# Turning the gathered rows of the expert part: TensorE and a copy from PSUM, or a transfer from tile to tile

## The chip, the core and the metric

The kernel runs on one core of a Trainium2 chip. The core has a matrix engine (TensorE, PE in the rows), three elementwise engines (VectorE or DVE, ScalarE or ACT, GpSimd or POOL), SyncE (SP), which here only issues transfers, and 16 DMA engines that carry out the transfers of all queues. Each engine runs its own instruction list in order; they meet through semaphores only. The metric is the device time of one execution in microseconds; lower is better.

## What is computed

One layer on 8 x 512 rows of 256 values: a modulated layer norm, a causal linear attention over 16 heads, a gated residual, a second modulated norm, and a mixture of 8 experts of which each row takes two. Cut to the part that matters here:

```
probs = softmax(xf @ router_w.T);  topv, topi = top_k(probs, 2);  topv = topv / (topv.sum() + 1e-9)
h   = gelu(einsum('td,edh->teh', xf, w1))        # D = 256, H = 1024, E = 8
y   = einsum('teh,ehd->ted', h, w2)
out = einsum('te,ted->td', cw, y)                # cw: the two shares of each row
x   = x + gb * out
```

## The kernel before

The kernel has two parts, one after the other. The first part (attention, second norm, router) walks over 32 chunks of 128 rows; it also splits each expert weight into a high and a low half of 16 bits, which stay in SBUF. It writes each normalised row, with its gate beside it, to `ffn_rows` in DRAM. A short piece between the parts sorts the rows by expert into `MAXB` = 71 blocks of 128 rows, each block of one expert.

The second, the expert part, runs 71 steps, one block each. For block m:

- GpSimd gathers 128 rows of `ffn_rows` into the slot `xg[q]` (8 slots, named `xt` and `stage` in the rows), 5 blocks ahead (`AHEAD`), and the shares with a second small gather.
- ScalarE's `row_high(m)` rounds the row's 256 values to 16 bits into `xs[:, m.p, 0:D]` (the tile `kstT`), VectorE's `row_low(m)` puts the remainder into `xs[:, m.p, D:2D]`. `m.p` is the parity of m: `xs` holds two blocks.
- TensorE's `xT(m)` transposes the four 128x128 pieces of it (`transpose_parts`, line 1172) into the PSUM bank `bank[7 * m.p]`; VectorE copies the bank to `x16[:, m.p, :]` (the tile `qstT`, line 716), two blocks as well.
- First product, W1 from here on (lines 1334 and 1336): 16 pairs of matmuls of 256 and 128 columns into `hidden`. ScalarE and VectorE add the parts, apply gelu and split the result in `amhi` and `amlo`.
- Second product, W2 (lines 1350 and 1352): 8 pairs of 512 and 256 columns. ScalarE and VectorE then form the gated row block, and GpSimd adds it into `out_dram` by an indirect transfer (line 919), each such transfer after the one before it has landed.

The order is written out by hand in `step_c` of each engine. TensorE's list in step a is `xT(a+1)`, W1(a), W2(a-1). Before W1(a) it waits for `xTe`, which VectorE raises after the copy of block a. VectorE's list in step a is: sum of W2(a-2), index copies, gated block a-2 (line 709), the copy of block a+1 (line 716), `row_low(a+2)` (line 687), two sums of W1(a) (line 723), two low halves (line 729). ScalarE's list is: the low part of W2(a-2), `row_high(a+2)`, two copies of W1(a), four gelus. ScalarE's `row_high(m)` waits for `xT` of block m-2, since it writes over that block's half of `xs`; VectorE's copy waits for `hB` of block m-2, the end of W1(m-2), since it writes over that block's half of `x16`. SyncE issues its last transfer, the shares to DRAM (line 1459), before the expert part begins and nothing in it.

Of the kernel before, what the change touches and what calls it, by code (L numbers as in the profile page):

```python
# [29 lines left out]
F16 = mybir.dt.float16  # L30
# [4 lines left out]
P = 128  # L35
B, S, D = 8, 512, 256
# [12 lines left out]
MAXB = (2 * T + E * (P - 1)) // P  # L49
# [51 lines left out]
def wait(eng, sem, value, most=None):  # L101

    if isinstance(value, int):
        if most is not None:
            value = min(value, most)
        if value <= 0:
            return
    eng.wait_ge(sem, value)


def adaln_block(nc, x, w_qkv, w_out, router_w, w1, w2, c_in, wmod, rope_cos, rope_sin, out):
    ctx = ExitStack()
    with ctx:
# [3 lines left out]
        def sem(name):  # L117
            return ctx.enter_context(nc.semaphore(name))
# [176 lines left out]
        s_g = [sem(f"s_g{q}") for q in range(GB)]  # L295
        s_h = [sem(f"s_h{q}") for q in range(GB)]
        s_shares = sem("s_shares")
        s_sc = sem("s_sc")

        x_rows = x.rearrange("b s d -> (b s) d")  # L300
# [21 lines left out]
        def steps_a(eng, step, order, after={}):  # L322


            for c in range(2 * CPB):
                step(At(0, c, CPB))
                if c in after:
                    after[c]()
            with eng.Fori(2, B - 1) as b:
                for c in range(CPB):  # L330
                    step(At(b, c, CPB))
            for c in range(CPB + max(lag for _, lag in order)):
                step(At(B - 1, c, CPB))

        def steps_c(eng, step):

# [58 lines left out]
        def _(dve):  # L395
# [289 lines left out]
            def row_low(m):  # L685
                wait(dve, c_["xh"], m.n + 1)
                v.tensor_tensor(xs[:, m.p, D:2 * D], xg[m.c % GB][:, 0:D], xs[:, m.p, 0:D], ALU.subtract)\
                    .then_inc(c_["xl"], 1)

            row_low(At(0, 0, UC))  # L690
            row_low(At(0, 1, UC))
            dve.wait_ge(c_["xT"], 1)
            v.tensor_copy(x16[:, 0, :], bank[0][:, 0:D].bitcast(F16)).then_inc(c_["xTe"], 1)

            def step_c(a):
                m = a.back(2)
# [8 lines left out]
                if m.inside(MAXB):  # L705
# [3 lines left out]
                    v.scalar_tensor_tensor(out=yw[:, m.p, :], in0=y_sum, scalar=share[:, q:q + 1],  # L709
                                           in1=xg[q][:, D:2 * D], op0=ALU.mult, op1=ALU.mult)\  # L710
                        .then_inc(c_["yw"], 1)
                m = a.back(-1)
                if m.inside(MAXB):
                    wait(dve, c_["xT"], m.n + 1)
                    wait(dve, c_["hB"], m.n - 1)
                    v.tensor_copy(x16[:, m.p, :], bank[7 * m.p][:, 0:D].bitcast(F16)).then_inc(c_["xTe"], 1)
                if a.back(-2).inside(MAXB):
                    row_low(a.back(-2))
                if a.inside(MAXB):
# [208 lines left out]
        def _(act):  # L928
# [108 lines left out]
            def row_high(m):  # L1037
                q, used = m.slot(GB)
                wait(act, s_g[q], 16 * (used + 1))
                wait(act, c_["xT"], m.n - 1)  # L1040
                copy(xs[:, m.p, 0:D], xg[q][:, 0:D]).then_inc(c_["xh"], 1)

            row_high(At(0, 0, UC))
# [27 lines left out]
        def _(pe):  # L1071
# [222 lines left out]
            last.then_inc(s_pe, 1)  # L1294


            def xT(m):
                wait(pe, c_["xl"], m.n + 1)
                wait(pe, c_["xTe"], m.n - 1)
                transpose_parts(bank[7 * m.p], xs[:, m.p, :]).then_inc(c_["xT"], 1)  # L1300

            pe.wait_ge(a_["whi"], NC)
            pe.wait_ge(a_["wlo"], NC)
            xT(At(0, 0, UC))
            pe.wait_ge(s_dve, marks["block_e"])

            expert, digits = {}, {}
# [6 lines left out]
            def step_c(a):  # L1314
# [3 lines left out]
                ahead = a.n + UC // 2  # L1318
                if ahead % UC == 0 and ahead < MAXB:
                    load_digits(ahead // UC)  # L1320
                if a.back(-1).inside(MAXB):
                    xT(a.back(-1))
                if a.inside(MAXB):
                    e = expert[a.n]
                    wait(pe, c_["xTe"], a.n + 1)
                    for mt in range(MT):
                        g, q = mt // 4, mt % 4
                        if q == 0:
# [32 lines left out]
        def _(sp):  # L1361
# [96 lines left out]
            sp.wait_ge(s_pool, marks["shares"])  # L1458
            sp.dma_start(share_d.rearrange("(p i) e -> p (i e)", i=NC), shares).then_inc(s_shares, 16)


# [1 line left out]
_INS = ["L0_attn_x", "L0_attn_w_qkv", "L0_attn_w_out", "L0_ffn_router_w", "L0_ffn_w1", "L0_ffn_w2",  # L1463
# [28 lines left out]
```

## Time and profile before

| | |
|---|---|
| median of 3 runs | 825.89 us (824.83 to 827.75) |
| the profiled execution | 825.53 us |
| its span in the trace | 823.2 us |
| TensorE busy | 737.3 us, 90% |
| VectorE, ScalarE, GpSimd busy | 81%, 71%, 62% |
| mean granted TensorE clock | 0.958 |

The span runs from the first to the last instruction of the trace; some 2.3 us of the execution lie outside it. The profile gives busy time by engine, and the same in 40 slices of the span, so that the two parts can be told apart: slices 1 to 18 are the first part, 19 and 20 the sorting, and 21 to 40 the expert part, from about 413 us on. A matmul is shown with the time from its start to its modelled end; several are under way at once, so that the distance between two starts, and not the duration, tells what one costs TensorE.

### The profile page before, as it was taken

The numbers are of one execution on the slowest core, as the hardware profiler recorded it, in microseconds if no ns is written. First come the engines' busy times: TensorE is split into PE (matmuls) and PEld (weight loads), VectorE is DVE, ScalarE is ACT, GpSimd is POOL, SyncE is SP. The second block draws the span as 40 slices with busy tenths as digits, with TensorE's granted clock in tenths as the row PEclk, the third lists the DMA queues.
The fourth block names the chain that finished last, engine by engine and source line by source line (L and its number), as shares of the span: only waits on it lengthen the run. The fifth ranks groups of instructions, "written<-read, shape, count | busy, mean of one in ns | idle before, by whom it ended". The sixth has DMA issues, their size and how long they took to land.

```text
span 823.2 us, 26404 instructions
## 1 busy us (share of the span) xinstructions
PE 737.3 (90%) x7949; PEld 540.3 (66%) x7949; DVE 663.8 (81%) x1488; ACT 580.3 (71%) x1103; POOL 514.3 (62%) x504
## 2 busy tenths in 40 slices
PE   6599999999999999973489999999999999999994
PEld 3366666666666666652367777777777777777772
DVE  2789999999999999965857777778777877777773
ACT  1478888888888888862057777777677767677762
POOL 3547576766666575744746666666676667667653
PEclk9799999999999999995589999999999999999998
DMA  6214333333333333310023333343334334343320
GB/s 207 86 41 126 107 115 111 107 108 105 111 113 114 109 116 115 112 53 32 21 79 75 73 71 69 68 78 70 73 73 76 66 69 78 66 76 70 74 31 0
DMA packets 52814, 68.78 MB, mean 84 GB/s; under 512 B 8864, under 2 KB 44080, under 8 KB 52736
## 3 DMA queue, kind: packets, MB, share of 16 engines
q0 software_dynamic: 18176, 27.06, 17.5%
q1 hardware_dynamic: 34560, 40.61, 16.0%
q8 instruction: 58, 0.95, 0.5%
q14 instruction: 20, 0.16, 0.1%
HBM read 46.50 MB, written 22.05 MB: 83 GB/s over the span
## 4 chain that ended last, share of the span: by engine, by line
PE 59%; DVE 16%; issue 10%; ACT 8%; POOL 3%; DMA 1%; DVEq 1%; another core or an unknown queue 0%; ACTq 0%; SPq 0%; POOLq 0%
PE hidden L1334 15%; PE bank L1350 15%; PE hidden L1336 8%; PE bank L1352 7%; PE bank L1189 5%; PE hidden L1172 3%; DVE amlo L511 2%; DVE nb L452 2%; PE bank L1172 2%; ACT feat L969 2%; ACT rb L968 2%; DVE rb L498 2%; DVE hT L475 2%; DVE st L432 2%; ACT qstT L932 1%
## 5 line engine op out<-in xcount | busy, mean ns | idle before, releaser
L1334 PE MATMUL hidden<-qstT,w1hi_k 128*128 128x256 f16 x1136 | 200.2, 274 | 1.1 <-DVE am L723 1.1
L1336 PE MATMUL hidden<-qstT,w1lo_k 128*128 128x128 f16 x1136 | 195.5, 220 | 0.0
L1350 PE MATMUL bank<-w,amhi 128*128 x568 | 188.6, 379 | 0.4
L1352 PE MATMUL bank<-w,amlo 128*128 x568 | 154.8, 273 | 0.0
L729 DVE TENSOR_TENSOR amlo<-am,amhi 128x512 f16<-128x512 f32 x142 | 98.4, 693 | 62.6 <-ACT am L1064 50.8
L919 POOL DMA_INDIRECT out_dram<-x,si x71 | 121.9, 1717 | 36.5 <-issue 27.4
L1334 PEld LDWEIGHTS hidden<-qstT,w1hi_k 128*128 x1136 | 111.7, 98 | 14.9 <-issue 1.3
L1336 PEld LDWEIGHTS hidden<-qstT,w1lo_k 128*128 x1136 | 111.7, 98 | 1.1
L1189 PE MATMUL bank<-wq,hT 128*128 128x256 f32 (+1 forms) x256 | 102.9, 528 | 9.2 <-DVE hT L475 9.1
L1063 ACT ACTIVATE amhi<-am 128x512 f16<-128x512 f32 x142 | 88.5, 623 | 12.6 <-DVE am L723 7.6
L1350 PEld LDWEIGHTS bank<-w,amhi 128*128 128x128 f16 x568 | 55.5, 98 | 62.3 <-issue 2.6
L1064 ACT ACTIVATE am<-am 128x512 f32<-128x512 f32 x142 | 87.5, 616 | 0.0
L900 POOL DMA_INDIRECT wq<-shares,gi x71 | 67.8, 955 | 22.1 <-issue 14.9
L511 DVE SCALAR_TENSOR_TENSOR amlo<-hidden,amhi 128x1024 f16<-128x1024 f32 x64 | 78.1, 1220 | 2.6 <-ACT amhi L994 2.3
L822 POOL CAST kst<-feat 128x512 f16<-128x512 f32 x32 | 19.5, 609 | 96.9 <-DVE feat L505 96.7
L932 ACT ACTIVATE feat<-hidden 128x512 f32<-128x512 f32 x71 | 42.4, 597 | 40.6 <-PE hidden L1336 36.3
L932 ACT ACTIVATE rb<-hidden 128x512 f32<-128x512 f32 x71 | 42.5, 598 | 38.8 <-PE hidden L1336 37.7
L1189 PEld LDWEIGHTS bank<-wq,hT 128*128 128x128 f32 x256 | 45.6, 198 | 36.3 <-issue 15.9
L994 ACT ACTIVATE amhi<-hidden 128x1024 f16<-128x1024 f32 x64 | 65.0, 1015 | 3.0 <-PE hidden L1135 1.5
L892 POOL DMA_INDIRECT xt<-ffn_rows,gi x36 | 40.4, 1122 | 41.2 <-DVE x L709 38.6
L892 POOL DMA_INDIRECT stage<-ffn_rows,gi x35 | 38.2, 1092 | 42.2 <-DVE x L709 30.7
L1352 PEld LDWEIGHTS bank<-w,amlo 128*128 128x128 f16 x568 | 55.6, 98 | 5.6
(203 smaller groups left out, 1814.2 us busy)
## 6 DMA issues: line engine op xcount, KB each, us to landing
stage<-in_L_ffn_w_dram SPq DMA_DIRECT2D x32, 512.0 KB, 4.1
xt<-in_L_attn_x_dram SPq DMA_DIRECT2D x32, 128.0 KB, 2.1
out_dram<-x SPq DMA_DIRECT2D x32, 128.0 KB, 1.7
ffn_rows<-h SPq DMA_DIRECT2D x32, 128.0 KB, 3.3
ffn_rows<-am SPq DMA_DIRECT2D x32, 128.0 KB, 3.1
am<-mod_rows SPq DMA_DIRECT2D x16, 128.0 KB, 3.6
mod_b<-mod_rows SPq DMA_DIRECT2D x8, 256.0 KB, 3.6
w<-in_L_wmod_dram SPq DMA_DIRECT2D x6, 256.0 KB, 4.4
```

The source lines that it names most:

```text
L511: v.scalar_tensor_tensor(out=amlo[:, g, :, :], in0=hidden[1][:, :, :], scalar=0.0, in1=amhi[:, g, :, :], op0=ALU.max, op1=ALU.subtract)\
L729: v.tensor_tensor(glo[:, a.p, h_], g32[:, a.p, h_], ghi[:, a.p, h_], ALU.subtract)\
L892: g.indirect_dma_start(xg[q], None, rows_d, bass.IndirectOffsetOnAxis(ap=gi[:, q, 0:1], axis=0)).then_inc(s_g[q], 16)
L919: g.indirect_dma_start(out_rows, bass.IndirectOffsetOnAxis(ap=si[:, m.c % GB:m.c % GB + 1], axis=0), yw[:, m.p, :], None, bounds_check=T - ...
L932: return v.activation(out_, in_, ACT.Copy, scale=scale)
L1063: v.activation(ghi[:, a.p, h_], g32[:, a.p, h_], ACT.Gelu, scale=1.0 / WS)
L1064: v.activation(g32[:, a.p, h_], g32[:, a.p, h_], ACT.Gelu, scale=1.0 / WS)\
L1189: last = t.matmul(dst, xT_[:, k * P:(k + 1) * P], w[k][:, lo], start=(k == 0), stop=(k == KT - 1))
L1334: t.matmul(dst.rearrange("p (q n) -> p q n", q=2), w1s[0][k][g][:, w_], both, start=(k == 0), stop=False)
L1336: last = t.matmul(dst[:, P:2 * P], w1s[1][k][g][:, w_], both[:, 0, :], start=False, stop=(k == KT - 1))
L1350: t.matmul(y[:, :], ghi[:, m.p, c_m], w2s[mt // 2][:, bass.ds(w_, 2 * D)], start=(mt == 0), stop=False)
L1352: last = t.matmul(y[:, D:2 * D], glo[:, m.p, c_m], w2s[mt // 2][:, bass.ds(w_, D)], start=False, stop=(mt == MT - 1))
```

## The change

For every block but the first, TensorE's four transposes and VectorE's copy are gone. In their place SyncE issues one transposing transfer, from `xs[:, m.p, :]` to `x16[:, m.p, :]`, SBUF to SBUF, 128 partitions by 512 values of 16 bits. SyncE waits for the same two things as before the two engines did together: `xl` of block m (its high and low values stand in `xs`) and `hB` of block m-2 (`x16` is free). The transfer raises `s_turn[m.p]` by 16 when it has landed. TensorE's W1(a) waits for that semaphore in place of `xTe`, and ScalarE's `row_high(m)` waits for it, of block m-2, in place of `xT`. Block 0 is turned as before, with VectorE's `row_low` of block 1 now behind the copy of block 0.

```diff
@@ steps
+        def turned(m):
+            return 16 * (m.pairs + m.p)
@@ VectorE
             row_low(At(0, 0, UC))
-            row_low(At(0, 1, UC))
             dve.wait_ge(c_["xT"], 1)
             v.tensor_copy(x16[:, 0, :], bank[0][:, 0:D].bitcast(F16)).then_inc(c_["xTe"], 1)
+            row_low(At(0, 1, UC))
...
-                m = a.back(-1)
-                if m.inside(MAXB):
-                    wait(dve, c_["xT"], m.n + 1)
-                    wait(dve, c_["hB"], m.n - 1)
-                    v.tensor_copy(x16[:, m.p, :], bank[7 * m.p][:, 0:D].bitcast(F16)).then_inc(c_["xTe"], 1)
@@ ScalarE, row_high(m)
-                wait(act, c_["xT"], m.n - 1)
+                before = m.back(2)
+                if isinstance(before.n, int) and before.n == 0:
+                    act.wait_ge(c_["xT"], 1)
+                elif before.inside(MAXB):
+                    wait(act, s_turn[before.p], turned(before))
@@ TensorE
-                if a.back(-1).inside(MAXB):
-                    xT(a.back(-1))
...
-                    wait(pe, c_["xTe"], a.n + 1)
+                    if a.n == 0:
+                        pe.wait_ge(c_["xTe"], 1)
+                    else:
+                        wait(pe, s_turn[a.p], turned(a))
@@ SyncE
+            def turn(a):
+                if not a.inside(MAXB) or (isinstance(a.n, int) and a.n == 0):
+                    return
+                wait(sp, c_["xl"], a.n + 1)
+                carry(sp)
+                wait(sp, c_["hB"], a.n - 1)
+                carry(sp)
+                sp.dma_start(x16[:, a.p, :].rearrange("p (j n) -> p j n", n=P), xs[:, a.p, :], transpose=True)\
+                    .then_inc(s_turn[a.p], 16)
+            steps_c(sp, turn)
```

TensorE's list between W2 of one block and W1 of the next, in the expert part. Before:

```order
L1350 MATMUL bank1<-w2_3,amhi 128x512
L1352 MATMUL bank1<-w2_3,amlo 128x256
L1172 MATMUL bank7<-ident16,kstT 128x128 [waits c_xTe,c_xl]
L1172 MATMUL bank7<-ident16,kstT 128x128 x3
L1334 ISA [waits c_sA,c_xTe]
L1334 MATMUL hidden0<-qstT,w1hi_k0_0 128x256
```

And now:

```order
L1351 MATMUL bank<-w_3,amhi 128x512
L1353 MATMUL bank<-w_3,amlo 128x256
L1335 ISA [waits c_sA,s_turn0]
L1335 MATMUL hidden<-qstT,w1hi_k_0 128x256
L1337 REGISTER_ALU
L1337 MATMUL hidden<-qstT,w1lo_k_0 128x128
```

Four transposes are gone from in front of W1, and W1's wait is for the transfer.

VectorE's list from the gated block to the first low half of a step, before:

```order
L709 SCALAR_TENSOR_TENSOR x1<-ra,wq,xt 128x256 [waits s_h0]
L716 COPY qstT<-bank7 128x512 [waits c_hB,c_xT]
L687 TENSOR_TENSOR kstT<-stage,kstT 128x256 [waits c_xh]
L723 TENSOR_TENSOR am<-hidden0,feat 128x512 [waits c_lA]
L723 TENSOR_TENSOR am<-hidden1,rb 128x512 [waits c_lB]
L729 TENSOR_TENSOR amlo<-am,amhi 128x512 [waits c_y,c_gA]
```

And now:

```order
L714 SCALAR_TENSOR_TENSOR x1<-ra,wq,xt 128x256 [waits s_h0]
L692 TENSOR_TENSOR kstT<-stage,kstT 128x256 [waits c_xh]
L723 TENSOR_TENSOR am<-hidden0,feat 128x512 [waits c_lA]
L723 TENSOR_TENSOR am<-hidden1,rb 128x512 [waits c_lB]
L729 TENSOR_TENSOR amlo<-am,amhi 128x512 [waits c_y,c_gA]
```

The copy out of PSUM, with its wait for TensorE, no longer stands between the gated block and `row_low`.

SyncE's list at its end, now (before, it ended with the shares):

```order
L1437 DMA ffn_rows<-am 128x256
L1460 DMA shares<-wq 128x256 [waits s_pool]
L1470 DMA_TRANSPOSE qstT<-kstT 128x4x128 [waits c_xl]
L1470 DMA_TRANSPOSE qstT<-kstT 128x4x128 [waits c_xl,c_hB] x6
L344 UNCONDITIONAL_BRANCH
```

The 70 transposing transfers stand behind all that SyncE did before, and in front of nothing.

## Rows read from the trace of the kernel before

**Rows 1.** The page: the span, busy time by engine, and TensorE in 40 slices.

```profile
span 823.2 us, 26404 instructions
PE 737.3 (90%) x7949; PEld 540.3 (66%) x7949; DVE 663.8 (81%) x1488; ACT 580.3 (71%) x1103; POOL 514.3 (62%) x504
...
PE   6599999999999999973489999999999999999994
```

**Rows 2.** Windows: busy time of each engine, granted clock, DMA share in the expert part.

```profile
core 0: us, PE busy (x) PEld busy (x) DVE busy (x) ACT busy (x) POOL busy (x), PEclk, DMA share, GB/s
440.00:800.00 360.00, 359.63 (x3385) 277.28 (x3383) 281.43 (x647) 258.26 (x520) 243.13 (x193) 1.00 0.38 70
```

**Rows 3.** The chain that ended last, 400 to 823 us, by line.

```profile
by line: PE hidden L1334 29.7%; PE bank L1350 28.7%; PE hidden L1336 14.8%; PE bank L1352 14.3%; PE bank L1172 3.6%; issue 1.7%; POOL mod_b L870 1.2%; another core or an unknown queue 0.9%; DMA xt<-ffn_rows,gi 0.9%; DMA out_dram<-x,si 0.6%;
```

**Rows 4.** Timeline of TensorE over one step: start, us, instruction.

```profile
601.81 0.22 PE L1336 MATMUL hidden<-qstT,w1lo_k 128*128 128x128 f16 x1
...
604.38 0.27 PE L1352 MATMUL bank<-w,amlo 128*128 x1
604.49 0.39 PE L1172 MATMUL bank<-ident,kstT 128*128 128x128 f16 x4
604.71 0.27 PE L1334 MATMUL hidden<-qstT,w1hi_k 128*128 128x256 f16 x1
...
607.35 0.38 PE L1350 MATMUL bank<-w,amhi 128*128 x1
...
609.95 0.39 PE L1172 MATMUL bank<-ident,kstT 128*128 128x128 f16 x4
610.18 0.27 PE L1334 MATMUL hidden<-qstT,w1hi_k 128*128 128x256 f16 x1
```

**Rows 5.** Timeline of VectorE and ScalarE in the same step.

```profile
601.40 0.42 DVE L716 COPY qstT<-bank 128x512 f16<-128x512 f16 x1
601.73 0.41 DVE L687 TENSOR_TENSOR kstT<-xt,kstT 128x256 f16<-128x256 f32 x1
...
605.01 0.69 DVE L729 TENSOR_TENSOR amlo<-am,amhi 128x512 f16<-128x512 f32 x1 [0.35 <-ACT am L1064]
605.40 0.39 ACT L932 ACTIVATE ra<-bank 128x256 f32<-128x256 f32 x1 [0.43 <-issue]
605.68 0.41 ACT L932 ACTIVATE kstT<-stage 128x256 f16<-128x256 f32 x1
```

**Rows 6.** TensorE line 1172 in the expert part: count, duration, first and last start.

```profile
L1172 PE MATMUL bank<-ident,kstT x284: 219/219/314, 413.1 to 798.3; 128*128 128x128 f16 x142
```

**Rows 7.** The page: SyncE's transfers, KB each, us from issue to landing.

```profile
stage<-in_L_ffn_w_dram SPq DMA_DIRECT2D x32, 512.0 KB, 4.1
...
out_dram<-x SPq DMA_DIRECT2D x32, 128.0 KB, 1.7
...
am<-mod_rows SPq DMA_DIRECT2D x16, 128.0 KB, 3.6
```

**Rows 8.** The page: the hardware queue; packets, MB, share of 16 engines' span.

```profile
q1 hardware_dynamic: 34560, 40.61, 16.0%
```

**Rows 9.** DMA queues, 540 to 780 us: the software queue, in the same columns.

```profile
q0 software_dynamic: 11141, 16.91, 38.3%
```

**Rows 10.** Timeline of the start of the expert part, TensorE and VectorE.

```profile
412.53 0.42 DVE L687 TENSOR_TENSOR kstT<-xt,kstT 128x256 f16<-128x256 f32 x1 [2.11 <-ACT kstT L932]
413.11 0.59 PE L1172 MATMUL bank<-ident,kstT 128*128 128x128 f16 x4 [7.67 <-DVE kstT L687]
413.90 0.43 DVE L687 TENSOR_TENSOR kstT<-xt,kstT 128x256 f16<-128x256 f32 x1 [0.94 <-ACT kstT L932]
414.25 0.42 DVE L693 COPY qstT<-bank 128x512 f16<-128x512 f16 x1
...
414.86 0.39 PE L1334 MATMUL hidden<-qstT,w1hi_k 128*128 128x256 f16 x1
...
421.05 0.28 PE L1334 MATMUL hidden<-qstT,w1hi_k 128*128 128x256 f16 x1 [1.12 <-DVE am L723]
```

More of the change, by code:

```diff
@@ L297, in adaln_block @@
         s_shares = sem("s_shares")
+        s_turn = [sem("s_turn0"), sem("s_turn1")]
         s_sc = sem("s_sc")
@@ L1294, in _ @@
             last.then_inc(s_pe, 1)
[L1297 to L1300, printed above, removed]
             pe.wait_ge(a_["whi"], NC)
             pe.wait_ge(a_["wlo"], NC)
-            xT(At(0, 0, UC))
+            wait(pe, c_["xl"], 1)
+            transpose_parts(bank[0], xs[:, 0, :]).then_inc(c_["xT"], 1)
             pe.wait_ge(s_dve, marks["block_e"])
```

## The prediction, made before the changed kernel ran

> **What bounds the kernel now.** I read the page first: TensorE is busy 90% of the span, and of the 40 slices all between 22 and 39 show 9 tenths or more [rows 1]. The change lies in those slices alone, so the windows come next. From 440 to 800 us TensorE is busy 359.63 of 360 us at a granted clock of 1.00, while VectorE has 281, ScalarE 258 and GpSimd 243 us of 360 [rows 2]. A busy share of 100% says only that some matmul is always under way. That it is also the bound is said by the chain that ended last: 91% of it from 400 us on lies on TensorE's five lines of the expert part [rows 3], and nothing else there but waits at the two ends holds 2%. So in this stage each microsecond taken out of TensorE's list is a microsecond of the kernel, until the next bound comes. The transposes, line 1172, hold 3.6% of 423 us, or 15.2 us.
>
> The timeline gives the same by steps. Line 1172 starts at 604.49 and again at 609.95: a step is 5.46 us. W1 begins 0.22 us after the transposes, W2 at 607.35, that is W1 takes 2.64 us, and W2 to the next transposes 2.60 us [rows 4]. 0.22 + 2.64 + 2.60 = 5.46: TensorE has no gap at all.
>
> **What is removed.** The trace has 284 transposes, 71 groups of four [rows 6]. Block 0 keeps its group. Of the other 70, that of block 1 stands right before W1(0), at 414.39 and still at the lower clock level (its matmuls last 0.61 us as a group against 0.39 later), and that of block 2 just before a gap of 1.12 us in which TensorE waits for VectorE anyway [rows 10]: worth nothing. So 68 groups count in full: 68 x 0.22 = 15.0 us. At the start the copy of block 0 no longer waits behind `row_low` of block 1: it can begin after 413.70, when the transposes of block 0 end, in place of 414.25, which lets W1(0) start some 0.4 us sooner. But the next thing of TensorE, at 421.05, waits for a sum of VectorE [rows 10], and I cannot see that all of the 0.4 reaches it; I take 0.2, between 0 and 0.4.
>
> VectorE loses a copy of 0.42 us a step (71 x 0.42 = 30 us of its busy time, line 716 in [rows 5]). VectorE doesn't set the end, so this is worth nothing by itself. `row_low` comes 0.33 us earlier, at 601.40 in place of 601.73, which matters below.
>
> **What is added: one transfer for each block, and its latency.** SyncE does nothing else in this part, so no other transfer is queued behind its waits. The transfer of block a+2 may start when `row_low(a+2)` is done and W1(a) has ended. In the step shown, the last matmul of W1(a) starts at 601.81 and lasts 0.22, to 602.03 [rows 4]; `row_low(a+2)` ended at 602.14 before and now ends at about 601.8 [rows 5]. So the end of W1(a), 602.03, releases the transfer. W1(a+2) begins at 610.18 now; with two groups of transposes fewer in between, at 610.18 - 0.44 = 609.74. **The transfer has 609.74 - 602.03 = 7.7 us** from SyncE's release to the last byte and TensorE's waking up. ScalarE also waits for it, before `row_high` (its call for block a+4), which comes about 1 us after W1(a+2) has started (605.68 against 604.71), so TensorE's wait always decides first.
>
> The trace of before has no transposing transfer; I bound it by its neighbours. Below: a plain 128 KB transfer issued by SyncE lands in 1.7 us [rows 7]. Above there are three steps. The plain one carries 1 KB a partition in one piece; a transposed tile has rows of 128 values, 256 bytes, so it needs at least 512 pieces, 32 for each of the 16 DMA engines in place of 8. The hardware queue's 34560 packets took 16.0% of 16 x 823.2 us, 61 ns each [rows 8]: 32 x 61 ns = 2.0 us in place of 0.5, so the landing comes to 1.7 + 1.5 = 3.2 us, or 3.6 + 1.5 = 5.1 us from the slowest 128 KB row [rows 7]. With the software queue's packet, 38.3% of 16 x 240 us over 11141 packets, 132 ns each [rows 9], the 32 pieces take 4.2 us and the landing 3.6 + 3.7 = 7.3 us. And if the tile were cut finer still, into pieces of 32 bytes (a 16-value edge), it would be 256 pieces an engine and 15.6 us. I take 4 us, near the 3.2 of the row for the same queue and size, because what counts in these rows is pieces and bytes, and both are known best there. All but the last of these bounds lie under 7.7 us, so the wait is covered in the forecast, with 3.7 us to spare. Its cover is W2(a-1), W1(a+1) and W2(a); if the transfer lasts longer, TensorE stands still by half of the excess in each step (two blocks are in flight).
>
> Beside the latency there is room on the DMA engines. They are busy 38% of a step [rows 2], 0.38 x 5.46 = 2.1 us. With 2.0 us more they would be busy 4.1 of 5.24 us: enough. GpSimd's list, 243 of 360 us, is 3.7 us of a step and has room for 5.24.
>
> The Trainium skill has a rule that speaks against the change. "VectorE: DVE Perf Modes", section "The three transpose paths", gives 1309 ns for a 128x128 16-bit transpose by the DMA crossbar and 390 ns for TensorE. An estimate from that page: four such pieces one after the other make 5.2 us of transfer, about the whole shortened step; a landing of 1.7 us as for a plain transfer added, 6.9 us would still be within the 7.7 us, but the DMA engines would be asked for 5.2 us beside their 2.1 us. The same notes say in "Advanced Engine Details and Errata", section "X-Bar Transpose (TRN2)", that such transfers are as fast as regular ones; by that the latency would be near the 1.7 us of the row. No row here shows a transpose by the crossbar, so these two only mark the ends.
>
> **The sum.** 825.5 - 15.0 - 0.2 = 810.3 us for the profiled execution, whose 825.53 is 0.36 below the median of 825.89. Against the median of the runs that is 810.7 us. With the start and the counted groups uncertain by some 2 us and code fetched at other places by as much, this case alone spans 806 to 814.
>
> **Rivals.**
>
> 1. *Slower: the DMA engines become the bound.* If a transposing transfer keeps them busy for D in each step, on top of the 2.1 us of the gathers and the scatter, the step is D + 2.1 once that is over 5.24, so from D = 3.1 us on, and it costs time against before from D = 3.4 us on. The place is TensorE's wait before W1. At the 132 ns of the software queue's packet, D = 4.2: a step of 6.3, 70 x (6.3 - 5.46) = 59 us more, 885 us. For it: D is the least known number here, and the gather, the share and the scatter would be slowed as well, of which the scatter of each block is issued only after the last one landed. Against it: the same queue's own packets are at 61 ns. The page with 1309 ns a piece belongs here: with its 5.2 us a step would be 7.3 us and the time 955 us. Pieces of 32 bytes would give 15.6 + 2.1 = 17.7 us a step, over 1600 us.
>
> 2. *The latency isn't covered.* W1(a+2) starts 2.64 + 0.16 us plus L after W1(a) starts, L being from release to wake; two steps then last 2.8 + L. From L = 7.7 us TensorE waits, from L = 8.1 the kernel is slower than before. L = 8.5 gives (2.8 + 8.5) / 2 = 5.65 us a step, 70 x 0.19 = 13 us more, 839 us. The highest bound but one above was 7.3 us, and SyncE's own time for issuing such a transfer comes on top; it is not in any row.
>
> 3. *No change.* TensorE's 0.22 us a step go, and another chain takes them: GpSimd's order of gather, share gather and scatter, or a loop through ScalarE. ScalarE is busy 3.9 us of 5.46, and waits several times a step [rows 2, 5]; nothing is near. Time as before, 826 us. The latency falling just at 8 us would look the same.
>
> 4. *It doesn't do what it says.* TensorE's list shows the transposes gone, SyncE's the transfers there; none.
>
> **Chances.** Forecast 0.60; DMA engines as the bound 0.21, of which a quarter under 870 us and a fifth beyond 960; latency just uncovered 0.11; no change 0.06; anything else 0.02. A measurement of this kernel tells about 0.3%, 2.5 us, from no change. Faster: the forecast and a little of the uncovered latency, 0.62. Same: 0.06. Slower: 0.32. The range runs from 806 us, the forecast's lower end, to 870 us: the forecast, no change, the uncovered latency and a quarter of the first rival, 0.60 + 0.06 + 0.11 + 0.05 = 0.82. The likeliest case's own range is 806 to 814.
>
> **What would show it.** Right: windows from 440 to 790 us with TensorE still busy at 99% or more at clock 1.00; line 1335 beginning 0.11 us after the last of line 1353, with no idle time before it; steps of 5.24 us; a row for the transposing transfer with a landing time under 7 us; a DMA share near 4.1 / 5.24 = 0.78. Wrong: idle time of TensorE before line 1335 released by the transfer into `qstT`. If the DMA share is then near 1, it is the first rival; if it is well below, the second. If TensorE waits before its line 1351 or ScalarE before its copies for anything else, the third. A TensorE that waits a good part of each step could also fall to the lower clock level, as it had after the gap of 7.67 us at 413 us [rows 10], though it kept the higher one over the gap of 1.12 us.

## The result, and the profile after

| | before | after |
|---|---|---|
| median | 825.85 us (824.83 to 827.75) | 843.87 us (841.34 to 847.02, 4 runs) |
| ratio | | 1.022, 95% interval 1.017 to 1.027 |
| profiled execution, its span | 825.53, 823.2 us | 847.02, 845.3 us |

The change makes the kernel 2.2% slower, by 1.7 to 2.7%; forecast was 1.8% faster. Here and below medians are taken over all executions, ratios over those in the faster of two states alone, so that the two can differ a little. The windows of the changed kernel from 440 to 800 us answer to [rows 2], with the same columns:

```profile
440.00:800.00 360.00, 348.72 (x2916) 253.23 (x2916) 244.00 (x548) 237.13 (x487) 220.19 (x183) 1.00 0.50 89
```

TensorE is busy 349 of 360 us in place of 359.63, at the same granted clock of 1.00, and every other engine is busy less as well: fewer blocks went through. The DMA share is 0.50, so the DMA engines are far from full. The page's line on the hardware queue answers to [rows 8]:

```profile
q1 hardware_dynamic: 72640, 49.80, 21.0%
```

38080 packets more than before on the hardware queue, 544 for each of the 70 transfers, and 21.0% of 16 x 845.3 us in place of 16.0% of 16 x 823.2: 733 us of one engine more, 19 ns a packet. SyncE's line 1470 in the expert part (ns: shortest, median, longest; first and last start in us):

```profile
L1470 SPq DMA_TRANSPOSE qstT<-kstT x70: 1189/1191/2617, 413.9 to 818.2; - x70
```

The first line of W1 in the page's costliest groups (busy us, mean ns of one, then the idle time just before them and what ended most of it):

```profile
L1335 PE MATMUL hidden<-qstT,w1hi_k 128*128 128x256 f16 x1136 | 219.5, 274 | 8.7 <-DVE am L723 4.7
```

SyncE takes 1.19 us to issue one. By the last packet of each in the trace it has landed 3.24 us after the start of the issue (median of 70; 9 in 10 under 4.24, the longest 5.39). The nearest of the 70 to being late has landed 1.39 us before the W1 that needs it starts, the median one 4.3 us before. And of TensorE's idle time before line 1335, 8.7 us, most (4.7) is ended by VectorE's sum. So the transfer is in time. Steps from the start of one W1 to the next last 5.89 us in the mean of 70 where 5.24 was forecast; 22 of them have 5.24, the others 5.3 to 7.6. In the kernel before the mean is 5.55, not the 5.46 of the one step that [rows 4] show: 52 of the 70 steps have 5.46 or less, the others up to 6.6.

The waits tell more. Both lists are of 440 to 800 us (engine, line, waited for; total, times, longest, in us). Before:

```profile
ACT rb L932 <- PE hidden L1336: 34.8, 61, 0.9
ACT feat L932 <- PE hidden L1336: 34.4, 53, 1.2
```

After:

```profile
...
ACT rb L932 <- remote: 27.5, 10, 3.9
DVE am L723 <- ACT rb L932: 24.0, 13, 3.8
ACT feat L932 <- remote: 22.5, 13, 3.6
```

TensorE raises three signals for the other engines in each step: hA at the end of the first half of W1, hB at the end of W1, and y at the end of W2. "remote" stands where no instruction of the profile ends near the moment of release. ScalarE's copy of W1's first half (`feat`) or second half (`rb`) waits 2 to 4 us for something that has no such end. One of these places, in order of the engines: TensorE, ScalarE, VectorE, GpSimd, SyncE (start, duration, instruction, idle before):

```profile
611.07 0.27 PE L1335 MATMUL hidden<-qstT,w1hi_k 128*128 128x256 f16 x1
...
613.70 0.27 PE L1335 MATMUL hidden<-qstT,w1hi_k 128*128 128x256 f16 x1 [0.33 <-issue]
...
614.26 0.22 PE L1337 MATMUL hidden<-qstT,w1lo_k 128*128 128x128 f16 x1
614.51 0.39 PE L1351 MATMUL bank<-w,amhi 128*128 x1
...
619.89 0.27 PE L1335 MATMUL hidden<-qstT,w1hi_k 128*128 128x256 f16 x1 [0.67 <-DVE am L723]
```

```profile
612.11 0.41 ACT L932 ACTIVATE kstT<-stage 128x256 f16<-128x256 f32 x1
615.38 0.60 ACT L932 ACTIVATE feat<-hidden 128x512 f32<-128x512 f32 x1 [2.85 <-remote]
618.43 0.60 ACT L932 ACTIVATE rb<-hidden 128x512 f32<-128x512 f32 x1 [2.46 <-remote]
```

```profile
613.66 0.42 DVE L692 TENSOR_TENSOR kstT<-stage,kstT 128x256 f16<-128x256 f32 x1
```

```profile
611.73 1.62 POOL L919 DMA_INDIRECT out_dram<-x,si  x1 [0.30 <-issue]
613.98 0.99 POOL L892 DMA_INDIRECT stage<-ffn_rows,gi  x1 [0.63 <-DVE x L714]
615.27 0.95 POOL L900 DMA_INDIRECT wq<-shares,gi  x1 [0.30 <-issue]
616.53 1.62 POOL L919 DMA_INDIRECT out_dram<-x,si  x1 [0.30 <-issue]
```

```profile
618.50 2.62 SPq L1470 DMA_TRANSPOSE qstT<-kstT  x1
```

W1 starts at 611.07 and its last matmul, at 614.26, ends at 614.48. The semaphore events of the trace put hA, due at 612.55, at 615.35, and hB, due at 614.48, at 618.41, 0.26 us after GpSimd's scatter at 616.53 has ended. TensorE has done its work in time and goes on to W2 at 614.51; only its signals come late. Everything that hangs on them follows: ScalarE, VectorE's sums, SyncE's transfer at 618.50, whose block had been ready in `xs` since 614.08, the end of VectorE's half of it (ScalarE's ended at 612.52), and TensorE itself at 619.89, in the middle of the next W1.

I call the time between the modelled end of the raising matmul and the semaphore event the *hold* of the signal. Counted over all signals from 440 to 790 us (hA, hB, and y at the end of W2), before has a mean hold of 0.20, 0.01 and 0.45 us and none over 2 us; after has 0.91, 0.62 and 0.70 us, and 13 over 2 us. Six of these 13 are alike: an hB that falls due while GpSimd issues the gather comes 0.1 to 0.3 us after the end of the scatter, 3.8 to 4.2 us late, as at 614.48. GpSimd issues gather, share and scatter there with 0.30 us between them.

### The profile page after: what moved, and what is told of

Its sections match the earlier page's. It is cut to its first block, busy times and chain, and to the rows that moved or that the text cites. A ratio compares the mean times of both kernels' runs of the same rounds, so it can differ in the third digit from the quotient of the medians.

```text
span 845.3 us, 25966 instructions
## 1 busy us (share of the span) xinstructions
PE 749.8 (89%) x7669; PEld 533.6 (63%) x7669; DVE 641.4 (76%) x1418; ACT 575.4 (68%) x1103; POOL 502.3 (59%) x504
## 3 DMA queue, kind: packets, MB, share of 16 engines
q1 hardware_dynamic: 72640, 49.80, 21.0%
## 4 chain that ended last, share of the span: by engine, by line
PE 53%; DVE 17%; issue 11%; ACT 9%; another core or an unknown queue 3%; POOL 3%; DMA 1%; DVEq 1%; ACTq 0%; SPq 0%; POOLq 0%
PE hidden L1335 15%; PE bank L1351 13%; PE hidden L1337 7%; PE bank L1353 6%; PE bank L1193 5%; PE hidden L1176 2%; DVE amlo L516 2%; DVE nb L457 2%; ACT feat L969 2%; ACT rb L968 2%; DVE rb L503 2%; DVE st L437 2%; DVE hT L480 2%; ACT qstT L932 1%
## 5 line engine op out<-in xcount | busy, mean ns | idle before, releaser
L1335 PE MATMUL hidden<-qstT,w1hi_k 128*128 128x256 f16 x1136 | 219.5, 274 | 8.7 <-DVE am L723 4.7
L1337 PE MATMUL hidden<-qstT,w1lo_k 128*128 128x128 f16 x1136 | 209.3, 219 | 2.5 <-issue 2.2
L919 POOL DMA_INDIRECT out_dram<-x,si x71 | 118.1, 1663 | 43.1 <-issue 23.6
L723 DVE TENSOR_TENSOR am<-hidden,rb 128x512 f32<-128x512 f32 x71 | 48.7, 686 | 32.7 <-ACT rb L932 26.4
L892 POOL DMA_INDIRECT xt<-ffn_rows,gi x36 | 36.0, 1000 | 63.2 <-DVE x L714 58.7
L723 DVE TENSOR_TENSOR am<-hidden,feat 128x512 f32<-128x512 f32 x71 | 48.8, 688 | 21.4 <-ACT feat L932 13.6
```

The lines of the kernel that those rows point to most:

```text
L723: v.tensor_tensor(four(dst), quarters(g)[:, :, 0, :], four(h_low[g]), ALU.add)\
L919: g.indirect_dma_start(out_rows, bass.IndirectOffsetOnAxis(ap=si[:, m.c % GB:m.c % GB + 1], axis=0), yw[:, m.p, :], None, bounds_check=T - ...
L1335: t.matmul(dst.rearrange("p (q n) -> p q n", q=2), w1s[0][k][g][:, w_], both, start=(k == 0), stop=False)
L1337: last = t.matmul(dst[:, P:2 * P], w1s[1][k][g][:, w_], both[:, 0, :], start=False, stop=(k == KT - 1))
```

## The experiments

All times are medians, with the shortest and the longest execution in parentheses; before, measured beside them, is 825.9 to 827.0 us. Each ratio is to before, with its 95% interval. "Spare tile" is one that the expert part doesn't use.

### 1. TensorE's shorter list without the transfer

```diff
-                        wait(pe, s_turn[a.p], turned(a))
+                        wait(pe, c_["xTe"], 2)
+                        wait(pe, c_["xl"], a.n + 1)
...
-            steps_c(sp, turn)
```

> The changed kernel without its transfer: SyncE issues nothing in the expert part, the first product of every block multiplies what stands in x16 from the start (that part of the computation is left out), and TensorE waits for row_low instead. Theory A, TensorE's list: between two waits TensorE's sequencer lives on the time that it runs ahead, and without the four transposes its list of register and matmul instructions no longer keeps up; then the loss is here too, 838 us or more. Theory B, the transfer: the list is fine, and a transfer under way on the DMA engines is what slows TensorE or its signals; then this gives the forecast of the change, 808 to 814 us.

814.79 us (813.49 to 815.86), ratio 0.986 [0.983, 0.989]. The gain of the shorter list is there: 12 of the 15 us, 0.8 us outside what theory B expected and far from theory A.

### 2. The transfers beside the kernel before

The kernel before, complete, with SyncE's transfers into a spare tile, and `row_high` waiting for them too.

> The kernel before, with the same 70 transposing transfers issued beside it into a tile that nobody reads; ScalarE's row_high waits for them, everything else runs as before. Theory A (TensorE's list): 825 to 828 us, the list is that of before. Theory B (the transfer under way): the loss of the change without its gain, 826 + 18 + 15, 850 to 862 us.

829.58 us (827.12 to 831.28), ratio 1.003 [1.001, 1.006]. 70 transfers as such cost 3 us here, which is 1.6 us above theory A and 20 below theory B: the transfer alone isn't the cause either.

### 3. A plain transfer

```diff
-                sp.dma_start(x16[:, a.p, :].rearrange("p (j n) -> p j n", n=P), xs[:, a.p, :], transpose=True)\
+                sp.dma_start(x16[:, a.p, :], xs[:, a.p, :])\
```

> The changed kernel with a plain transfer of the same bytes from tile to tile in place of the transposing one (the rows are not transposed, that part of the computation is left out). Theory A (TensorE's list): as changed, 841 to 847 us. Theory B, if any transfer does it: 841 to 847 us too; if only the transposing form does it, by its 544 small packets: 808 to 814 us.

850.25 us (837.64 to 850.88), ratio 1.021 [1.011, 1.030]. No execution is near 808 to 814, though the page now has 44640 packets on the hardware queue in place of 72640, the issue takes 0.46 us and the landing 1.67. Neither the turning, nor the number of packets, nor the latency is what costs the time; either of the two transfers does it.

### 4. After, with TensorE's transposes kept as spare work

> The changed kernel, with TensorE's four transposes of each block kept as spare work whose result nobody reads. Theory A (TensorE's list): 825 to 828 us, TensorE has its slack back. Theory B (the transfer under way): 850 to 862 us.

852.22 us (844.2 to 857.17), ratio 1.033 [1.029, 1.037]. With TensorE's list as long as before it is no faster, as theory B had it; it differs from experiment 2 in VectorE's missing copy and in TensorE's wait for the transfer.

### 5 and 6. No scatter

The changed kernel and the kernel before, each without GpSimd's indirect add into the output (line 919).

```diff
-                    g.indirect_dma_start(out_rows, bass.IndirectOffsetOnAxis(ap=si[:, m.c % GB:m.c % GB + 1], axis=0),
-                                         yw[:, m.p, :], None, bounds_check=T - 1, oob_is_err=False,
-                                         compute_op=ALU.add).then_inc(s_sc, 16)
```

> The changed kernel without GpSimd's scatter in the expert part (the gated blocks are formed but not added to the output; that part of the computation is left out). Theory C: while GpSimd issues the scatter, TensorE's signals hA and y, and at times its own instruction list, are held until that issue ends, as nearly every late hA and y of the traces falls into such an issue; with the step at 5.24 us and the transfer in the loop these holds feed each other. Then the loss goes with the scatter: 805 to 814 us. Theory D: the transfer's own place in the loop (end of W1, transfer, W1 two blocks on) costs the time, whatever GpSimd does: 835 us or more, as only the scatter's time at the very end is saved.

> The kernel before without GpSimd's scatter (that part of the computation is left out), as the measure for the run without the scatter of the changed kernel. Both theories: TensorE is the bound at 5.46 us a step, so 818 to 824 us, the few slow steps and the last scatter's landing saved. The difference to the changed kernel without scatter is then the gain of the change alone: 12 to 15 us by theory C, a loss by theory D.

After: 805.24 us (804.32 to 807.42), ratio 0.975 [0.973, 0.977]. Before: 819.07 us (818.27 to 821.22), ratio 0.992 [0.990, 0.994]. Both are as theory C expected. **Without the scatter the change gains 13.8 us, close to the 15.2 of the forecast.** Taking the scatter away is worth 7 us to the kernel before and 39 us to the changed one. It takes away GpSimd's issue and the scatter's traffic on the DMA engines at once (their share from 440 to 780 us is 0.34 in place of 0.50), so these two aren't told apart. The waits of 440 to 780 us show the signals on time again:

```profile
ACT rb L923 <- PE hidden L1328: 45.4, 62, 1.0
...
ACT feat L923 <- PE hidden L1328: 38.6, 62, 0.6
```

Without the scatter GpSimd pauses some 3 us in each step. It has no pause near the end of the part, where it issues the last share gathers one behind the other, and there both kernels have late signals after all, the only ones over 0.9 us (3 and 2). In the kernel before without scatter, which has no transfer either, GpSimd and ScalarE:

```profile
776.73 0.94 POOL L899 DMA_INDIRECT wq<-shares,gi  x1 [0.30 <-issue]
777.98 0.94 POOL L899 DMA_INDIRECT wq<-shares,gi  x1 [0.30 <-issue]
```

```profile
781.42 0.60 ACT L923 ACTIVATE feat<-hidden 128x512 f32<-128x512 f32 x1 [3.08 <-remote]
```

hA, due at 777.36, comes at 781.40. So a hold of 4 us needs neither the scatter as such nor a transfer: it came with six indirect issues 0.30 us apart. The same count for the two main kernels (issues at most 0.4 us apart taken as one row of issues): of the signals held over 0.9 us, 11 of 11 before and 60 of 61 after fall due inside such a row or less than 0.3 us ahead of it.

### 7. Four tiles in place of two

SyncE's wait for `hB` goes two blocks back (`a.n - 3`), so that a late hB no longer delays the transfer.

> The changed kernel with four buffers of turned rows in place of two (the other two lie in a tile that the expert part doesn't use), so that a transfer waits for the end of W1 four blocks back, which is always past. Theory D (the loop from hB through the transfer back to W1 costs the time): 808 to 820 us. Theory C (the holds act on hA and y, which this leaves as they are): 836 us or more.

853.52 us (848.59 to 862.98), ratio 1.031 [1.028, 1.034]. As theory C expected, the loop from hB over the transfer to W1 isn't it.

### 8. Transfers beside, and TensorE not waiting for them

Experiment 1 with the transfers added, into a spare tile.

> As e_none (no transposes on TensorE, x16 left as it stands, which leaves out that part of the computation), but with the 70 transposing transfers issued into a spare tile, and ScalarE's row_high waiting for them; TensorE waits for row_low and not for the transfer. Theory C: at a step of 5.24 us the transfers beside are enough to bring on the holds, 830 us or more. Theory D: TensorE doesn't wait for them, so 813 to 820 us.

847.74 us (840.79 to 859.19), ratio 1.031 [1.023, 1.038], against 814.79 of experiment 1. TensorE doesn't wait for the transfer, ScalarE's `row_high` does but has no idle time for it in the list of waits, and it still costs 33 us. So the wait for it isn't the cause, its presence is; but beside the kernel before it cost 3.

### 9. The missing copy, taken out of experiment 2

As experiment 2, less VectorE's copy; TensorE keeps its transposes and doesn't wait for the transfer. Blocks from the second on are computed from what the tile holds at the start.

> The kernel before with the transfers beside it (into a spare tile), less VectorE's copy: TensorE keeps its transposes and waits for no transfer (blocks from the second on are computed from what stands in the tile at the start). If VectorE's copy is what separates the 829.6 of that kernel from the 852 of the one in which both the copy is gone and TensorE waits for the transfer: 845 to 855 us. If it is TensorE's wait for the transfer: 826 to 832 us.

856.31 us (846.01 to 873.23), ratio 1.036 [1.029, 1.043]: the copy, not TensorE's wait, is what separates 829.6 from 852.

### 10 and 11. A spare copy of VectorE put back into the changed kernel

```diff
+                if a.back(-1).inside(MAXB):
+                    v.tensor_copy(spare16, bank[0][:, 0:D].bitcast(F16))
                 if a.back(-2).inside(MAXB):
                     row_low(a.back(-2))
```

> The changed kernel with a copy of VectorE of the same size (128x512 out of PSUM, 0.42 us) put back at its old place, writing a spare tile that nobody reads. If the missing copy is what turned the small loss (transfers beside the old kernel: 829.6) into the large one, because VectorE's later operations moved against GpSimd's scatter: 820 to 832 us. If it is TensorE's shorter step: unchanged, 840 to 850 us.

> The changed kernel with a spare VectorE copy of 128x512 values of 16 bits at the old place as in the run before, but from SBUF to SBUF instead of out of PSUM, some 0.2 to 0.4 us. If the delay in VectorE's list is what helped: 820 to 832 us, in proportion to the copy's time. If the access to PSUM is what helped: 840 us or more.

Out of PSUM: 823.27 us (820.11 to 828.33), ratio 0.996 [0.994, 0.999]. From SBUF to SBUF: **819.12 us (817.64 to 821.3), ratio 0.992 [0.990, 0.995]**. Both kernels are complete. Work that nobody needs, added to the changed kernel, takes 21 to 25 us off it and brings it under the kernel before. TensorE's row in the windows of 440 to 780 us, with the SBUF copy:

```profile
440.00:780.00 340.00, 339.31 (x3008) 255.38 (x3007) 261.96 (x624) 247.47 (x500) 227.55 (x187) 1.00 0.54 97
```

No signal is held over 2 us in either. The copy from SBUF takes 0.29 us, that from PSUM 0.42: the shorter one gives more, so the gain isn't in proportion to the copy's time, as had been expected. What the copy does must be that it moves something in time.

### 12 and 13. The transfer alone delayed

VectorE's list as in the changed kernel; SyncE waits besides for the first (sA) or the second sum (sB) of block a. The edit for sA:

```diff
                 wait(sp, c_["hB"], a.n - 1)
                 carry(sp)
+                wait(sp, c_["sA"], a.n - 1)
+                carry(sp)
```

> The changed kernel, complete; SyncE waits in addition for VectorE's first sum of block a (sA) before it issues the transfer of block a+2. VectorE's list is as in the changed kernel. The transfer is issued some 1 us later in the step (3.3 to 4.3 us after the start of W1(a)) and with 3.2 us of landing still comes before W1(a+2) at 10.5. If VectorE's copy helped because it delayed the transfer: 818 to 830 us. If it helped by moving VectorE's own work: unchanged, 840 to 850 us.

> The same with the second sum (sB), so that the transfer is issued some 1.7 us later than in the changed kernel, about 5 us after the start of W1(a), with 2 us left before TensorE needs it. If the delay of the transfer is what counts: 812 to 830 us. If VectorE's own work: 840 to 850 us.

sA: 829.95 us (823.74 to 839.5), ratio 1.004 [1.002, 1.006]. sB: 823.78 us (819.02 to 829.62), ratio 0.997 [0.993, 1.001]. Issued 0.4 and 0.9 us later in the step than in the changed kernel (medians after W1's start: 3.57 us, then 3.93 and 4.44), the transfer costs 14 and 20 us less. The shifts are smaller than the 1 and 1.7 us expected. With VectorE's list as it is in the changed kernel, moving the transfer alone gives most of the loss back.

### 14. row_low behind the two sums

> The changed kernel, complete, with row_low of block a+2 in VectorE's list behind the two sums of block a in place of ahead of them; no spare copy. The transfer comes later by some 2 us, and the sums no longer stand behind row_low. If the delay of the transfer counts: 812 to 830 us. If the sums' being later is what helped with the spare copy: 840 us or more.

839.86 us (822.46 to 846.26, 4 runs), too far apart for a ratio: one execution fits the first expectation, two fit the second. 12 of its hB signals are held over 0.9 us. A later transfer isn't enough by itself, then; this run I can't explain by the transfer's place.

### 15 and 16. The scatter moved in GpSimd's order

The changed kernel with the order scatter, gather, share, and with gather, scatter, share.

> The changed kernel, complete, with one edit on GpSimd: in each step it issues the scatter first, and the gather and the share gather behind it (before: gather, share, scatter). The scatter then starts about 0.3 us after the gated block is ready, 2.8 us earlier in the step than now. Theory C (TensorE's signals are held while GpSimd issues the scatter, 1.62 us): the place of the scatter in the step decides. 1.4 to 3.0 us after the start of W1 it covers the end of W1 (hB), which in this kernel lets both VectorE's second sum and SyncE's transfer go; W2's end and hA are free. Expected 815 to 835 us, other than 844 by more than 5. If the hold were no matter of where the scatter stands but only of how busy GpSimd and the queues are: unchanged, 840 to 848 us.

> The changed kernel, complete, with the scatter between the gather and the share gather: it starts about 1.3 us after the gated block is ready, and would cover 2.7 to 4.3 us of the step, between the end of W1 (2.6) and the end of W2 (5.2). Theory C: no signal of TensorE falls inside, so this is the best place of the three, 808 to 815 us, near the 805 of the kernel without scatter and the 811 of the forecast. The rival (only GpSimd's and the queues' load counts): 840 to 848 us.

Scatter first: 831.89 us (826.68 to 835.15), ratio 1.006 [1.004, 1.009]. In between: 828.4 us (823.4 to 838.03), ratio 1.001 [0.998, 1.004]. Both take 12 to 15 us off the changed kernel. With the scatter first the time is as expected and the reason isn't: y is no longer held with the scatter first (0.02 us in the mean), but hA, expected free, is (0.83 us), and hB (0.47 us). That the middle place would be free of signals, 808 to 815 us, was wrong. Note the windows with the scatter first, and then those of experiment 1:

```profile
440.00:780.00 340.00, 339.01 (x2910) 251.10 (x2909) 240.76 (x544) 233.73 (x486) 227.01 (x183) 1.00 0.51 94
```

```profile
440.00:780.00 340.00, 339.50 (x3029) 256.30 (x3030) 255.76 (x568) 249.28 (x506) 229.30 (x189) 1.00 0.38 73
```

The two have nearly the same busy time of TensorE, 99.7 and 99.9%, but the first has 4% fewer matmuls. In such kernels the pairs of W1 often start 0.22 us apart where they start 0.165 apart elsewhere, as in the timeline of the changed kernel from 613.70 on: one distance in five is 0.2 to 0.3 us with the scatter first, one in fourteen in experiment 1, one in four in the changed kernel. The modelled durations, 0.27 and 0.22 us, cover the difference. Why the pairs come slower isn't shown.

### 17. The gather held back until hB is out

For the last experiment I sorted the signals of all kernels above. W1's end, hB, is often due close to the start of the gather (counted: from 0.3 us before it to 1.0 after). If hA had come by 0.25 us before the gather began, hB was held over 0.9 us in no case of 612. If hA was still out by then, hB was held in 65 cases of 73. So TensorE's signals seem to queue up: what hasn't left when GpSimd's next row of issues begins leaves at the end of it. The rule was found in these traces, so it needs a run of its own. This edit forbids the case:

```diff
                 if m.inside(MAXB):
+                    wait(pool, c_["hB"], a.n + 1)
                     gather(m)
```

> The changed kernel, complete, with one more wait on GpSimd: before the gather of step a it waits for hB of block a, the end of W1(a), so that neither hA nor hB can still be on its way when GpSimd begins its next gather, share and scatter. The wait costs GpSimd only time that it has idle (it is busy some 3.9 us of a step). If the backlog of TensorE's signals over the gather is what turns the gain into a loss: no hB is held over 0.9 us any more, and 812 to 828 us. If it is a symptom only: 838 to 850 us.

834.75 us (833.09 to 836.14), ratio 1.010 [1.007, 1.013]: 9 us better than the changed kernel, and no hB is held over 0.9 us, as expected; but not the 812 to 828. The wait ties GpSimd to TensorE, so that hA now falls due inside the scatter in 56 of 61 steps:

```profile
602.51 1.62 POOL L920 DMA_INDIRECT out_dram<-x,si  x1 [0.30 <-issue]
```

```profile
604.54 0.60 ACT L933 ACTIVATE feat<-hidden 128x512 f32<-128x512 f32 x1 [1.49 <-PE hidden L1338]
```

The scatter's issue ends at 604.13, `feat` starts at 604.54. hA's mean hold is 1.48 us. The run takes all holds over 2 us away and gives 9 us back, so they are only a part of the loss. That the rest lies in the holds of 1 to 2 us is my reading; the new wait also binds GpSimd to TensorE, and no run separates the two.

### The kernels side by side

Holds of all signals, read from the semaphore events of 440 to 790 us of each profiled execution. Its time stands in parentheses, since it can lie 10 us from the median. Some events are missing from the traces, most of all those of y in experiment 17 (25 of 61).

| kernel | median us (profiled) | mean hold hA, hB, y | held over 2 us |
|---|---|---|---|
| before | 825.9 (825.5) | 0.20, 0.01, 0.45 | 0 |
| before, transfers beside (2) | 829.6 (829.3) | 0.43, 0.02, 0.57 | 0 |
| the same, less VectorE's copy (9) | 856.3 (846.0) | 0.68, 0.32, 0.71 | 7 |
| after | 843.9 (847.0) | 0.91, 0.62, 0.70 | 13 |
| after, transposes kept (4) | 852.2 (844.2) | 0.66, 0.36, 0.75 | 7 |
| after, no transfer (1) | 814.8 (813.5) | 0.54, 0.03, 0.39 | 0 |
| the same, transfers beside (8) | 847.7 (840.8) | 0.81, 0.49, 0.43 | 9 |
| after, four tiles (7) | 853.5 (863.0) | 1.04, 0.84, 0.68 | 17 |
| after, spare copy (10, 11) | 823.3, 819.1 (820.1, 817.6) | 0.58, 0.02, 0.41 and 0.52, 0.02, 0.41 | 0, 0 |
| after, transfer later (12, 13) | 830.0, 823.8 (823.7, 823.9) | 0.68, 0.04, 0.61 and 0.70, 0.10, 0.60 | 0, 1 |
| after, gather waits for hB (17) | 834.8 (834.0) | 1.48, 0.14, 0.01 | 0 |

Of the others, experiment 3 has 15, 14 has 13, 15 has 4, 16 has 13, and the two without scatter 3 and 1. Every kernel with 7 or more such holds takes 839 us or more, but for experiment 16, at 828.4; every one with 4 or fewer takes under 835. That goes together; it doesn't say which causes the other.

## Why the prediction was wrong

**What bounds the kernel.** "In this stage each microsecond taken out of TensorE's list is a microsecond of the kernel, until the next bound comes" was right: without the scatter the same edit gained 13.8 us, and without the transfer 12. The next bound was the error. I looked for one in busy shares and in lengths of loops, and found none near. What came, as far as the runs show it, is how promptly TensorE's signals reach the others, and that has no row of its own. It was there before the change: the 70 steps of the kernel before take 6.6 us more than 70 times the 5.46 of the step shown, about the 7 us that go with the scatter.

**What is removed.** 15.0 us for the transposes: 13.8 measured (experiments 5 and 6), the start's 0.2 us included. VectorE's copy was costed at nothing, with `row_low` 0.33 us earlier as the only consequence, a harmless one. **This is the step that failed**, together with the transfer's own term, which was also nothing as long as the landing stayed within 7.7 us. Each is nearly right alone: without transfers the kernel that lacks the copy is 12 us faster (experiment 1), and beside the kernel before the transfers cost 3 us. Where both apply, it isn't so: with the transfers there, taking the copy out costs 27 us (experiment 2 against 9), and with the copy gone, the transfers cost 33 us (experiment 1 against 8). The copy kept the transfer at a place in the step where it did little harm. Taken out of experiment 2, it turns 829.6 into 856.3 us; put back into the changed kernel, in a form that does nothing, it turns 843.9 into 823.3 or 819.1 us.

**What is added.** The landing was taken at 4 us, with bounds from 1.7 to 15.6; it is 3.2 us. SyncE's issue, which I had said was in no row, is 1.19 us and is contained in it. The slack of 7.7 us was never used up: at least 1.39 us of it were left in each step. That one of my bounds also read 3.2 us is luck: it priced 32 pieces an engine at 61 ns, the trace has 34 at some 20 ns, and the issue of 1.19 us wasn't in the sum. The Trainium skill, "VectorE: DVE Perf Modes", "The three transpose paths", led to an estimate of 6.9 us for four pieces with the landing; the trace has 3.24, so the pieces don't run one after the other. By the Trainium skill's other rule ("Advanced Engine Details and Errata", "X-Bar Transpose (TRN2)") it would be as fast as a plain one; the trace has 1.67 us for the plain transfer of the same tile (experiment 3), so the turning one takes twice as long, and the measurement decides.

**DMA engines.** Their share is 0.50, not 0.78, since a transfer of 544 packets keeps them busy for some 0.7 us a step (the hardware queue has 11.8% of the 16 engines from 540 to 780 us, with 40 transfers) in place of 2.0. I had scaled by a mean packet of far larger transfers. Rival 1 falls with D = 0.7 where it needed 3.4.

**Rival 2** named 839 us, near the result, for a latency from 8.1 us; with 3.2 us it falls too, and experiment 8 is slow with no wait of TensorE for the transfer at all. A rival that names the time and not the mechanism isn't right.

**Rival 3** spoke of GpSimd's order and of ScalarE's waits, "nothing is near". Its sign, ScalarE waiting before its copies, is the one that came. ScalarE's waits were the place where the trace of before could have shown it: where y fell due while GpSimd was in line 919 it was held 0.62 us in the mean (41 times, up to 1.3), and hA 0.32 us (32 times, up to 0.75); outside it 0.1 and 0.06 us. I read the waits for their sums only, and these were idle time of an engine that has some to spare.

**The range.** 843.9 us lies between 806 and 870 all the same. That is luck: the upper part of the range was there for busy DMA engines and an uncovered latency, and neither came. Of its lower part, no run shows the 2 us that the sum allows for code fetched at other places.

**The mechanism, as far as it is shown.** Three things are needed for the whole loss, each with a run that lacks it: GpSimd's scatter (5), the transfer (1), and a place in the step that VectorE's copy or a later issue avoids (10 to 13). The direct sign is a TensorE signal that comes 1 to 4 us behind its matmul, after a row of GpSimd's indirect issues; 7 of the 13 longest come within 0.3 us of the end of a scatter's issue. What the scatter adds to such a row may be its place in it and not its kind, as the share gathers without it show (5 and 6). Late hA and hB make ScalarE and VectorE late, until TensorE waits for the sums, as at 619.89. That late signals also bring GpSimd's next burst nearer to the next signal, so that one hold leads to another, is my reading of the timelines and was not tested alone. **What stays open** is what, in the chip, holds the signals, and why a transfer issued about 0.2 us after the start of the gather (median in the changed kernel 0.15 us, experiment 4 0.19, experiment 9 0.24, experiment 8 -0.05) is so much worse than one at 0.4 or later (experiments 2 and 10 0.47, 11 0.38, 12 0.80, 13 1.54). Experiment 14, at 1.95 us and still slow, and experiment 8 at -0.05 say that this offset isn't the whole rule. Nor do the holds carry the whole loss: experiment 17 takes the long ones away and gives 9 us back, and experiment 16 has as many over 2 us as the changed kernel and is 15 us faster.

## What to carry to other kernels

Before an instruction is costed at nothing because its engine isn't the bound, look at what starts at its end: here a transfer moved by 0.3 us into a worse place against GpSimd's issues, and that cost more than the whole edit gained. Price what is removed and what is added together, not each by itself. Compare, for the bounding engine's signals, the end of the last instruction with the start of its first reader, near the issue of indirect transfers above all; a group that waits for "remote" is the sign. And where a change that should gain loses, try delaying the new transfer before giving the change up: one more wait on SyncE brought back 20 us (18 had been lost), and the best version here, with a dummy copy, is 0.8% faster than the kernel before.

## What the runs showed of the hardware

- While GpSimd issued an indirect scatter of 128 rows (1.62 us), TensorE's signals that fell due then came up to 1.3 us late in the kernel before, and up to 3.5 us late in the changed one, with a transfer of SyncE in each step. The longest hold of the changed kernel, 4.2 us, is that of an hB due during the gather; it came 0.18 us after the scatter's end. TensorE itself went on working. Without scatters the mean was under 0.1 us, but behind six gathers issued 0.30 us apart a signal was 4.0 us late without scatter and transfer.
- A transposing transfer of 128x512 values of 16 bits, SBUF to SBUF: 1.19 us of SyncE, 544 packets, landed 3.24 us after the start of the issue (median). The plain one: 0.46 us of SyncE, 144 packets, 1.67 us.
- TensorE's busy time was 99.7% in a kernel that ran 4% fewer matmuls in the same stretch. The count beside the busy time is the number to compare.
